# Graph network on one core: the first layer's message product over two PSUM banks, VectorE's and ScalarE's orders rewritten, own products one step later, weights loaded earlier

## The reference

```python
h = mish(concat([x[src], x[dst], edge_attr]) @ W1 + b1)
messages = mish(h @ W2 + b2)
agg = segment_sum(messages, dst, num_segments=n)
u = mish(concat([x, agg]) @ W3 + b3)
y = x + (u @ W4 + b4)
y = (y - mean(y)) * rsqrt(var(y) + 1e-5) * gamma + beta
x = layernorm(x + y)
# the next layer's first two products, on this x:
#   x @ W_l  (later summed over neighbours) and  x @ W_r + b_l
```

## Time and profile before

| | |
|---|---|
| median of 3 runs | 1387.11 us (1385.57 to 1390.77) |
| the profiled execution | 1386.91 us |
| its span | 1385.1 us |
| PE busy | 1256.2 us, 91% |
| DVE, ACT, POOL busy | 1024.6, 857.5, 677.2 us |
| mean granted PE clock | 0.963 of full speed |

### The profile page before, as it was taken

How to read it: one execution, slowest core, us unless ns; L and a number is a source line. 1 busy time by engine, 2 the same in 40 slices (tenths; PEclk the granted TensorE clock), 3 DMA queues, 4 the chain that set the end, 5 groups by cost and what they waited for, 6 DMA issues and landing times. The chain is left out here.

```text
span 1385.1 us, 18735 instructions
## 1 busy us (share of the span) xinstructions
PE 1256.2 (91%) x5872; PEld 1004.6 (73%) x5872; DVE 1024.6 (74%) x1809; ACT 857.5 (62%) x772; POOL 677.2 (49%) x475
## 2 busy tenths in 40 slices
PE   2964999999999999999999997887799896998997
PEld 2853777777777777777777775665587775887886
DVE  3222799999999999999999999445677247756335
ACT  1224999999999999999999997245523002211111
POOL 0017787888888888888888841125300000011000
PEclk9986999999999999999999999999899997999999
DMA  5768877777777777777777752386200510000001
GB/s 194 255 225 174 178 148 133 162 147 157 152 152 147 161 150 152 154 151 157 148 154 154 145 107 45 98 275 212 95 1 0 205 66 1 17 1 1 1 16 60
DMA packets 99178, 171.52 MB, mean 124 GB/s; under 512 B 34338, under 2 KB 39632, under 8 KB 99112
## 3 DMA queue, kind: packets, MB, share of 16 engines
q0 software_dynamic: 70000, 103.83, 38.7%
q1 hardware_dynamic: 26768, 62.22, 13.2%
q10 hardware_dynamic: 2344, 4.63, 1.0%
HBM read 133.34 MB, written 37.11 MB: 123 GB/s over the span
## 5 line engine op out<-in xcount | busy, mean ns | idle before, releaser
L503 POOL DMA_INDIRECT G<-q_dram,idx_all x168 | 349.1, 2078 | 54.5 <-issue 43.7
L807 PE MATMUL ps_x<-wA_hi,hT_hi 128*128 128x512 f32 x668 | 270.4, 405 | 1.3 <-DVE hT_lo L579 1.3
L807 PE MATMUL ps_x<-wA_hi,hT_lo 128*128 128x512 f32 x668 | 264.4, 396 | 0.0
L807 PE MATMUL ps_x<-wA_lo,hT_hi 128*128 128x512 f32 x668 | 264.2, 395 | 0.0
L495 POOL DMA_INDIRECT G<-p_dram,idx_all x168 | 173.8, 1034 | 149.2 <-issue 146.6
L807 PEld LDWEIGHTS ps_x<-wA_hi,hT_hi 128*128 128x128 f32 x668 | 125.7, 188 | 34.0 <-issue 1.7
L807 PEld LDWEIGHTS ps_x<-wA_hi,hT_lo 128*128 128x128 f32 x668 | 125.5, 188 | 30.2
L807 PEld LDWEIGHTS ps_x<-wA_lo,hT_hi 128*128 128x128 f32 x668 | 125.5, 188 | 28.4
L586 DVE TENSOR_TENSOR x<-ps_x,b 128x512 f32<-128x512 f32 x167 | 113.7, 681 | 26.0 <-PE ps_x L807 25.7
L769 PE MATMUL ps_x<-ident,G 128*128 128x128 f32 x672 | 103.3, 277 | 31.4 <-DMA G<-q_dram,idx_all 23.7
L769 PEld LDWEIGHTS ps_x<-ident,G 128*128 128x128 f32 x672 | 85.6, 143 | 55.0 <-DMA G<-q_dram,idx_all 24.2
(11 more groups left out here) (286 smaller groups left out, 2889.7 us busy)
## 6 DMA issues: line engine op xcount, KB each, us to landing
ea_raw<-in_eaT SPq DMA_DIRECT2D x84, 128.0 KB, 4.4
adj_dram<-adj_sb POOLq DMA_DIRECT2D x42, 210.2 KB, 9.7
adj_dram<-zeros SPq DMA_DIRECT2D x11, 640.5 KB, 4.5
U_lo<-adj_dram SPq DMA_DIRECT2D x10, 640.0 KB, 6.3
adjT_dram<-adjT_sb SPq DMA_DIRECT2D x10, 640.0 KB, 6.0
adjT_rest<-adjT_dram SPq DMA_DIRECT2D x7, 640.0 KB, 10.0
w_raw_g<-in_w SPq DMA_DIRECT2D x4, 1024.0 KB, 7.4
agg_dram<-agg_sb POOLq DMA_DIRECT2D x42, 84.0 KB, 9.3
```

The lines of the kernel that those rows point to most:

```text
L503: g.indirect_dma_start(G[:, b.slot, c * D:(c + 1) * D], None, q_dram, bass.IndirectOffsetOnAxis(ap=idx_all[:, i:i + 1], axis=0), compute_o ...
L807: last = t.matmul(ps_x2[c % 2][:, :], h[:, b.slot, e], w[:, k, :], start=(k == 0 and i == 0), stop=(k == KD - 1 and i == 2))
```

## The change

- Message products alternate between two banks: `ps_zm = [ps_Tx[1], ps_out]`; product r waits for Z of product r - 2.
- ACT in a message step: adjacency copy, high part, weight quarter, then sigmoid and arctan of the tile before. The first two u casts go ahead of the last sigmoids.
- DVE in a message step: Z, weight quarter, degree, low part of the next tile.
- SINES is (0, 4, 8, R). POOL's last group waits for the first new x.
- W3's lower half, b4, gamma and beta are loaded by SP at the end of the edge phase, and W4 as soon as W3's upper half is split; the raw weight buffer w_raw is now one with the edge phase's gather buffer G. W3's lower half is split a quarter per x tile.
- LAG is 3: next products one step on, and from tile 7 the new x is turned ahead of the own product of the tile before. W_r is split one step on, the degrees in steps 1, 3, 4, 5.
- Small tiles of graph_layers live in b4, its vectors in b3, gam and bet.

```diff
-SINES = (0, 5, 9, R)
+SINES = (0, 4, 8, R)
-LAG = 2
+LAG = 3
+DEGREES = (0, 2, 3, 4)
...
@@ edge_phase, SP's end
                 sp.dma_start(w3_raw, by_slices(w03[0:D, :])).then_inc(w3_in, 16)
                 sp.dma_start(b3[:, :], bcast(b03)).then_inc(b3_in, 16)
+                sp.dma_start(raw[1], by_slices(w03[D:2 * D, :])).then_inc(w3b_in, 16)
+                for t, b in ((b4, b04), (gam, g0), (bet, be0)):
+                    sp.dma_start(t[:, :], bcast(b)).then_inc(vec_in, 16)
+                sp.wait_ge(w3_lo, KD)
+                sp.dma_start(raw[0], by_slices(w04)).then_inc(w4_in, 16)
...
+        ps_zm = [ps_Tx[1], ps_out]
...
@@ first_layer, ACT
-                act.dma_start(raw[1], by_slices(w03[D:2 * D, :])).then_inc(w3_in, 16)
-                act.dma_start(b4[:, :], bcast(b04)).then_inc(b4_in, 16)
                 for r in range(ZE, R):
                     x_high(r)
-                    if r == ZE + 2:
-                        act.dma_start(raw[0], by_slices(w04)).then_inc(w4_in, 16)
-                        act.wait_ge(w3_in, 16)
-                        for k in range(KD):
-                            split_high(wB_hi, raw[1], k, w3_hi)
+                    if r > ZE:
+                        if r == ZE + 1:
+                            act.wait_ge(w3b_in, 16)
+                        split_high(wB_hi, raw[1], r - ZE - 1, w3_hi)
...
-                    if r == R - 1:
-                        u_high(0)
+                    if r >= R - 1:
+                        u_high(r - R + 1)
+                    if r >= 1:
+                        act.wait_ge(z_ready, r)
...
+                        a.activation(TH[:, cols(r - 1)], Z[r - 1][:, :], ACT.Sigmoid, scale=-1.0).then_inc(sig, 1)
...
@@ first_layer, POOL
                     wait(t_ready, i + 1)
+                    if r1 == R:
+                        wait(x_new, 1)
                     u_of(r0)
...
@@ first_layer, DVE
-                        v.tensor_tensor(Z[r - 1][:, :], ps_out[:, :], Z[r - 1][:, :], ALU.add).then_inc(z_ready, 1)
-                    if r + 1 < R:
-                        low(r + 1)
+                        v.tensor_tensor(Z[r - 1][:, :], ps_zm[(r - 1) % 2][:, :], Z[r - 1][:, :], ALU.add).then_inc(z_ready, 1)
...
                         v.tensor_reduce(deg[:, r:r + 1], adj_in[:, r % SLOTS, :], AX.X, ALU.add).then_inc(d_ready, 1)
-                    if r == R - 1:
-                        u_low(0)
-                u_low(1)
+                    if r + 1 < R:
+                        low(r + 1)
+                    else:
+                        u_low(r - R + 1)
...
+                    if R - LAG <= n < R:
+                        low_of(slot(Ta_lo, n), ps_nT, slot(Ta_hi, n), n_hi, n + 1, n_lo)
...
@@ first_layer, PE
-                    else:
-                        pe.wait_ge(z_ready, r)
+                    if r >= 2:
+                        pe.wait_ge(z_ready, r - 1)
                     pe.wait_ge(lo_ready, r + 1)
-                    three_products(nc, ps_out, slot(Ta_hi, r), slot(Ta_lo, r), wB_hi, wB_lo, True, True).then_inc(z_out, 1)
+                    three_products(nc, ps_zm[r % 2], slot(Ta_hi, r), slot(Ta_lo, r), wB_hi, wB_lo, True, True).then_inc(z_out, 1)
+                pe.wait_ge(z_ready, R - 1)
...
+                        if R - LAG - 1 <= n < R - 1:
+                            turn_n(n + 1)
```

More of the change, by code:

```diff
@@ L153, in gnn @@
         wA_hi, wA_lo = sb("wA_hi", [P, KD, D], F32R), sb("wA_lo", [P, KD, D], F32R)
-        b3 = sb("b3", [P, D])
+        b3, b4, gam, bet = (sb(n, [P, D]) for n in ("b3", "b4", "gam", "bet"))
+        with ExitStack() as raws:
+            w_raw = sb("w_raw", [P, 2 * KD, D], F32, raws)
+        adjT_held = sb("adjT_held", [P, 2 * KD * D])
+        w3b_in, w4_in, vec_in = (sem(n) for n in ("w3b_in", "w4_in", "vec_in"))
         edge_sems, edge_numbers = [], top.enter_context(ExitStack())
@@ L190, in gnn @@
         adj_held = [sem(f"adj_held{u}") for u in range(HELD)]
-        first_layer(nc, sb, pb, sem, edge_sems, ident, half_pi, eps_col, X, U_hi, U_lo, Y, w_raw, w_hi, w_lo, b3, deg, rdeg, nrdeg, has, slow,
-                    agg_dram, adj_dram, adjT_dram, w03, w04, b04, g0, be0, w1l, b1l, w1r, adjT_held, adj_held)
+        first_layer(nc, sb, pb, sem, edge_sems, ident, half_pi, eps_col, X, U_hi, U_lo, Y, w_raw, w_hi, w_lo, b3, b4, gam, bet, deg, rdeg, nrdeg, has, slow,
+                    agg_dram, adj_dram, adjT_dram, w1l, b1l, w1r, w3b_in, w4_in, vec_in, adjT_held, adj_held)
         edge_numbers.close()
@@ L451, in passes @@
             return n
-        w3_raw = G[:, 0, :].rearrange("p (k d) -> p k d", d=D)
+        raw = [w_raw[:, i * KD:(i + 1) * KD, :] for i in range(2)]
+        w3_raw = raw[0]
         def place(r):
@@ L1011, in _ @@
                 for r in range(R + 1):
-                    if r >= 1:
-                        act.wait_ge(z_ready, r)
-                        act.sem_inc(turn, 1)
-                        a.activation(TH[:, cols(r - 1)], Z[r - 1][:, :], ACT.Sigmoid, scale=-1.0).then_inc(sig, 1)
-                        act.wait_ge(sig, r)
-                        act.sem_inc(turn, 1)
-                        a.activation(TH[:, cols(r - 1)], TH[:, cols(r - 1)], ACT.Arctan).then_inc(atan, 1)
                     if r < R:
@@ L1033, in _ @@
                         split_high(wC_hi, raw[1], r - KD, wl_hi)
-                    if r == R - 1:
-                        u_high(0)
+                    if r >= R - 1:
+                        u_high(r - R + 1)
+                    if r >= 1:
+                        act.wait_ge(z_ready, r)
+                        act.sem_inc(turn, 1)
+                        a.activation(TH[:, cols(r - 1)], Z[r - 1][:, :], ACT.Sigmoid, scale=-1.0).then_inc(sig, 1)
+                        act.wait_ge(sig, r)
+                        act.sem_inc(turn, 1)
+                        a.activation(TH[:, cols(r - 1)], TH[:, cols(r - 1)], ACT.Arctan).then_inc(atan, 1)
                     for r0, r1 in zip(SINES, SINES[1:]):
@@ L1054, in _ @@
                         root(0, s)
-                    if s == 0:
+                    if s == 1:
                         act.wait_ge(wr_in, 16)
@@ L1078, in with_beta @@
                     g.tensor_tensor(Z[r][:, :], X[:, cols(r)], bet[:, :], ALU.add).then_inc(xe_ready, 1)
-                for t, b in ((gam, g0), (bet, be0)):
-                    g.dma_start(t[:, :], bcast(b)).then_inc(gb_in, 16)
                 wait(w3_lo, KD)
                 g.dma_start(raw[1], by_slices(w1l)).then_inc(wl_in, 16)
-                wait(b4_in, 16)
-                wait(gb_in, 32)
+                wait(vec_in, 48)
                 g.tensor_tensor(bet[:, :], bet[:, :], b4[:, :], ALU.subtract).then_inc(b_diff, 1)
@@ L1269, in turn_u, with turn_n @@
                     turned(ps_Tx[r % 2], TH[:, cols(r)], u_T)
+                def turn_n(n):
+                    pe.wait_ge(x_new, n + 1)
+                    if n >= 1:
+                        pe.wait_ge(n_lo, n)
+                    turned(ps_nT, X[:, cols(n)], n_T)
                 turn_x(ZE)
@@ L1301, in _ @@
                     n = s - LAG
-                    if n >= 0:
-                        pe.wait_ge(x_new, n + 1)
-                        if n >= 1:
-                            pe.wait_ge(n_lo, n)
-                        turned(ps_nT, X[:, cols(n)], n_T)
+                    if 0 <= n < R - LAG:
+                        turn_n(n)
                     if 1 <= s < R - 1:
@@ L1345, in graph_layers @@
 def graph_layers(nc, sb, pb, sems, ident, eps_col, X, U_hi, U_lo, Y, w_hi, w_lo, rdeg, nrdeg, has, slow,
-                 adjT_held, adj_held, adjT_dram, vec0, g1, be1, w21, b21, w22, b22, w31, b31, w32, b32, out):
+                 adjT_held, adj_held, adjT_dram, vec, spare, g1, be1, w21, b21, w22, b22, w31, b31, w32, b32, out):
     with ExitStack() as ctx:
@@ L1355, in graph_layers, with part @@
         y, tmp, t_be = (sb(n, [P, 2, D], F32, ctx) for n in ("y_n", "tmp_n", "t_be"))
-        vec = [vec0, *(sb(f"vec{i}", [P, D], F32, ctx) for i in (1, 2))]
-        ones = sb("ones", [P, P], F32, ctx)
-        gcol, bcol = sb("gcol", [P, KD], F32, ctx), sb("bcol", [P, KD], F32, ctx)
-        st_c, mv_c = sb("st_c", [P, KD, R * 6], F32, ctx), sb("mv_c", [P, KD, 2], F32, ctx)
-        sd_c, sc_c, ms_c, sh_c = (sb(n, [P, KD], F32, ctx) for n in ("sd_c", "sc_c", "ms_c", "sh_c"))
-        st, mv = sb("st_n", [P, 2, 6], F32, ctx), sb("mv_n", [P, 2, 2], F32, ctx)
-        sd, rs = sb("sd_n", [P, 2], F32, ctx), sb("rs_n", [P, 2], F32, ctx)
-        keep = sb("keep", [P, R], F32, ctx)
+        used = [0]
+        def part(n):
+            used[0] += n
+            assert used[0] <= D
+            return spare[:, used[0] - n:used[0]]
+        ones, keep = part(P), part(R)
+        st_c, mv_c = (part(KD * n).rearrange("p (k i) -> p k i", k=KD) for n in (R * 6, 2))
+        st, mv = (part(2 * n).rearrange("p (u i) -> p u i", u=2) for n in (6, 2))
```

(2 more changed lines are left out.)

47 lines of the change are left out of this document (21 added, 26 removed).

## The result

| | before | changed |
|---|---|---|
| median of 4 runs | 1386.75 us | 1373.29 us (1370.8 to 1375.8) |
| the profiled execution | 1386.91 us | 1373.94 us |
| its span | 1385.1 us | 1372.3 us |
| mean granted PE clock | 0.963 | 0.969 |

The ratio to the kernel before is 0.9902, 95% interval 0.9884 to 0.9920: 13.5 us faster, where 18.8 were forecast. It lies inside the range, and closest to the rival in which every store lands late (1374.5).

What follows compares the result with a forecast made beforehand. Messages were taken as bound by a 6.43 us ACT and DVE cycle between Zs, PE waiting. Gains 0.9 + 12.0 + 5.5 + 2.9, less 1.9 and 0.6, make 18.8 us off 1386.91: forecast 1368, range 1361.5 to 1377.

Steps and rivals of the forecast that it cites:

- the rival in which every store lands late: Messages: crowded queues make all stores land as the slowest did, 8.4 us; time 1374.5, chance 0.24.
- The cut cycle and the new bound: Messages: the 6.43 us cycle through the sigmoid is cut; the two-slot adjacency store then paces, 5.6 us a step.
- part (b): Message steps, product 0 to 9: 49.2 us where it was 61.2, a gain of 12.0 us.
- part (a): x products: spread weight quarters and two fewer DMA issues on ACT start the first message product about 0.9 us earlier.
- Part (c): Message product 9 to the first y_in: 6.7 us where it was 12.2, a gain of 5.5 us.
- Part (d): First y_in to u product 4: 27.85 us where it was 30.7, a gain of 2.9 us.
- Part (e): u product 4 to the end: 6.0 us more work against 4.1 of idle time regained, a loss of 1.9 us.
- The clock: PE: remaining waits may make a product run at 1.2 GHz; 0.6 us off the gain, between 0 and 2.5.
- The table loads: ACT: a switch costs 1.3 us; with the skill's 1.38 us drain, four would be some 5 us dearer, time near 1373.
- The free store (1363): Messages: the store does not bind, pace falls to the chain's 4.55 us a step; time 1363, chance 0.17.
- the case in which the change does nothing in the messages: Messages: another wait keeps 6.4 us a step, only 7.4 us are won elsewhere; time 1380, chance 0.06.

Runs made afterwards that it cites:

- experiment 1: Changed kernel with SP issuing the store of the adjacency copy ahead of the ring's read: 1371.61 us, ratio 0.9899.
- experiment 5: Changed kernel with the store ahead of the ring's read and all ten b4 additions on POOL done before the message steps: 1363.84 us, ratio 0.9839.
- experiment 2: Changed kernel with POOL adding b4 to the first five tiles of X early, ahead of the load of W_l: 1369.34 us, ratio 0.9884.
- experiment 12: Changed kernel with loads of W3's lower half, b4, gamma, beta, W4 back in the first layer on ACT, W3's lower quarters split together: 1372.53 us.
- experiment 7: Changed kernel with the casts of u 0 and u 1 on ACT at their old places: 1377.09 us, ratio 0.9936.
- experiment 11: Changed kernel without POOL's wait for the first new x ahead of its last group: 1376.37 us, ratio 0.9932.
- experiment 8: Changed kernel without the early turn of the new x, turned at the start of its own step: 1376.21 us, ratio 0.9931.
- experiment 9: Kernel of experiment 5 with, besides, DVE's low part of the next tile ahead of quarter and degree: 1362.18 us, ratio 0.9821.
- experiment 6: Changed kernel with LAG 2 again, W_r's splits and the degrees one step earlier, early turn of the new x kept: 1377.49 us, ratio 0.9936.

## Why the prediction was right or wrong

- **The cut cycle and the new bound: right.** The sigmoid's way out of the cycle, the store with two slots as what paces next, and its place behind the degree are shown by the copies' waits and by experiments 1 and 5. The store's issue lay 4.8 us behind its copy in steps 2, 3, 4 and 5 (930.55 - 925.75 = 4.8), as worked out. It was not the only bound: without the wait for it 2.1 us were won (experiment 1).
- **The size of part (b): wrong, 7.9 us instead of 12.0.** The step that failed is "POOL ... shares time with DVE's quarters then, also in that wait": it looked at POOL's work behind the sine and not at its additions of b4 in step 0, which part (a) moves 2.5 us later, ahead of no wait at all. Taking them away wins 2.6 us, in experiment 2 and in experiment 12. That a quarter beside the additions takes 2.42 us stood in the trace before, at 941.24. The rest is landings. On the chain that ends at copy 7, forecast at 35.6 us from copy 1 and measured at 39.8 (955.92 - 916.14), store 1 was issued 1.5 us late (6.3 us behind its copy instead of 4.8), which is step 0's delay, and stores 1, 3 and 5 took 7.1, 10.8 and 5.9 us to land, 2.8 more than the 6.3, 6.3 and 8.4 entered. I put the longest beside the read of W_l; in both kernels it was beside the read of W_r.
- **Part (a): right as a term, wrong as a whole.** 0.9 us came, and went again one stage later.
- **Part (c): right in size, half right in the path.** 5.5 us, to the tenth of the 6.7 expected; experiment 7 shows that the casts carry it, less 2.3 us at the root. But PE is busy for all of the 6.70 us (the row of 965.20 above), with product 9, a turn and u product 0, and that product is what y_in waits for. ACT's chain, the one I added up, ends with u 1's low part at 971.78, 0.2 us before y_in starts at 971.97. Two paths of equal length gave the number, and a shorter chain on ACT alone could not have beaten it.
- **Part (d): right in sum** (27.55 for 27.85), and its steps too: 8.6 for 8.8, 7.0 for 7.05, 12.0 for 12.0 (the terms given for the last add up to 11.8). POOL's wait was entered at 1.5 us and is worth 2.85. It did not remove the contention but moved part of it: in the second step, counted as free of it, y_out took 1.61 us. That this step still came out at 7.0 is luck, as experiment 11 shows.
- **Part (e): too small a loss, 3.5 instead of 1.9.** Of the 4.6 us of idle time I counted 4.1 as regained. Some 1.2 of it was the end of the stage, which stays, and one wait for a low part remains, 1.1 us at 1060.93. So 2.4 us of idle time are left, where the prediction looked for under 1. Parts (d) and (e) together were to win 1.0 us and lost 0.4.
- **The clock** cost less than the 0.6 us entered, in this profile. Product 1 took 4.37 us, but copy 2 behind it waited for its store anyway, and the u product of 981.37 took 5.46 us inside a norm step that DVE set. It can cost more: in the profile of experiment 8 product 1 took 5.49 us, copy 2 waited for PE and not for its store, and the messages took 55.7 us.
- **The table loads.** Two loads lie in ACT's chain to u 1's low part, which stands ahead of y_in on DVE: the sine starts at 964.28 behind the load of 962.99, the sigmoid at 969.20 behind that of 967.90, 1.3 us each. By the drain of 1.38 us beside each load that the Trainium skill states ("ScalarE: Activation LUTs", "What ACT_TABLE_LOAD costs") that low part would have ended 2.8 us later, and the first y_in would have come 2.6 us later, by my estimate; the trace does not bear the page out here.
- **The rivals.** The free store (1363) was not what happened: it is what experiments 5 and 9 had to make, and they came to 1363.8 and 1362.2. "All stores land late" gave nearly the measured time, but only in part for its reason: the six stores in traffic landed 0.8 us later (7.1), not 2.1; the rest came from POOL's additions and part (e). Of the case in which the change does nothing in the messages, one piece is true: one bank instead of two can't be told from nothing.
- **A sum:** PE's idle time in the earlier trace rows adds up to 31 us, not 30; nothing hung on it.

## What to carry to other kernels

When a bound is cut, list every wait that was shorter than the old step and cost each with all that is queued ahead of it; here a store behind a ring read behind a reduction became the pace. Bounds of about equal length hide each other: an edit that removes one may measure as little or nothing (the low part's order won 1.7 us of message time alone and lost it again, and 4.25 behind the two other edits; the store first won 2.1, where a new slow quarter took its place), so test them together before dropping one. And when a change moves work in time, look for what another engine does at the new moment, and whether the old trace already shows such a meeting.

## What the runs showed of the hardware

The slowing of DVE by POOL was stronger than I had taken it to be. A 128x512 subtraction of two SBUF operands takes 0.68 us alone. Beside POOL's five additions of b4 it took 3.21 us, 3.85 in experiment 1 and 2.42 before, and ended each time about 0.55 us behind POOL's last addition: it can last as long as POOL's batch does. Beside POOL's work on u it was less: 0.74 and 1.34 us in the changed kernel (947.47 and 952.28, POOL busy from 945.14 to 955.98), and four together in experiment 6 took 6.39 us instead of 2.47. In the same stretches DVE's subtraction that reads PSUM stayed at 0.68 us (910.36, POOL busy until 916.83) and the SBUF reduction of the degree at 1.48 (944.52 in experiment 1, POOL busy from 941.54 to 951.98).

The granted clock showed a scatter of its own: the first x product took 3.0 us in eight of the twelve profiles up to experiment 11 and 4.6 in four, with the same wait before it, which moves the x stage from 20.2 to 21.7 us. That may be part of the 5 us between the fastest and the slowest run of the changed kernel; it is why a single profile tells a term of 1 us only by the stretch in which it lies, and in the messages not even there.
